# Tree stage of an eight-stage kernel: leaf nodes by gathered rows instead of dense products

## The reference, cut to what matters

```
logits = layernorm(x) @ W_in.T + b_in            # [tokens, 8 * 255]
acts   = silu(logits)
node 0 of each tree is visited; from a visited node the path goes left or right
by logits > 0, seven times; dmap is 1 at the eight visited nodes, else 0
x = x + (acts * dmap) @ W_out.T
```

## Time and profile before

| | us |
|---|---|
| median of 3 runs | 1630.63 (1630.32 to 1631.8) |
| profiled execution, its own time | 1630.92 |
| its span, first to last instruction | 1629.2 |
| PE busy | 1438.7 (88%) |
| DVE busy | 1072.1 (66%) |
| ACT busy | 755.6 (46%) |
| POOL busy | 116.5 (7%) |

### The profile page before, as it was taken

How to read it: one execution, slowest core, us unless ns; L and a number is a source line. 1 busy time by engine, 2 the same in 40 slices (tenths; PEclk the granted TensorE clock), 3 DMA queues, 4 the chain that set the end, 5 groups by cost and what they waited for, 6 DMA issues and landing times.

```text
span 1629.2 us, 26350 instructions
## 1 busy us (share of the span) xinstructions
PE 1438.7 (88%) x9842; PEld 1074.1 (66%) x9849; DVE 1072.1 (66%) x2358; ACT 755.6 (46%) x1264; POOL 116.5 (7%) x168
## 2 busy tenths in 40 slices
PE   7999999878897996799989999999988889999557
PEld 5666666557783443477786878787764677788446
DVE  4455575778877874687866465655458988886344
ACT  2211212257773666376672222222224877788323
POOL 1000000000000000111000000000010011001323
PEclk9999999989998997899998999999998999999779
DMA  9462202320000000000008910000100000010166
GB/s 323 167 207 78 78 1 78 127 85 14 14 3 0 1 1 1 25 14 1 14 2 265 303 43 1 1 1 0 33 7 7 1 7 2 7 31 24 41 186 180
DMA packets 60285, 96.62 MB, mean 59 GB/s; under 512 B 11091, under 2 KB 48972, under 8 KB 59982
## 3 DMA queue, kind: packets, MB, share of 16 engines
q1 hardware_dynamic: 57742, 78.50, 15.0%
q10 hardware_dynamic: 544, 12.16, 2.2%
q0 software_dynamic: 1872, 4.27, 0.7%
HBM read 73.21 MB, written 37.30 MB: 68 GB/s over the span
## 4 chain that ended last, share of the span: by engine, by line
PE 50%; issue 18%; DVE 15%; ACT 6%; DVEq 4%; DMA 2%; SPq 1%; POOL 1%; ACTq 1%; POOLq 1%
PE bank L1997 8%; PE bank L1998 8%; PE bank L1689 7%; PE bank L1667 7%; DVE MB L927 3%; PE bank L1794 3%; DVE plo L945 2%; PE bank L1845 2%; PE bank L1595 1%; PE bank L1765 1%; PE bank L1799 1%; PE bank L1798 1%; DMA jx<-copy_routed 1%; DVE raw L1211 1%; PE bank L1767 1%
## 5 line engine op out<-in xcount | busy, mean ns | idle before, releaser
L945 DVE TENSOR_TENSOR plo<-e,phi 120x512 f16<-120x512 f32 x256 | 179.1, 705 | 50.2 <-ACT phi L1419 46.5
L1413 ACT ACTIVATE e<-bank 120x512 f32<-120x512 f32 x256 | 150.6, 588 | 42.7 <-PE bank L1799 34.3
L927 DVE TENSOR_REDUCE MB<-bank 128x4 bf16<-128x480 f32 x256 | 155.9, 646 | 15.1 <-PE bank L1767 11.5
L1419 ACT ACTIVATE phi<-e 120x512 f16<-120x512 f32 x256 | 161.2, 630 | 8.8
L1344 ACT ACTIVATE act<-bank,bin 127x512 f32<-127x512 f32 x64 | 43.1, 687 | 167.2 <-DVE dec L757 163.2
L1667 PE MATMUL bank<-xT,winT 128*127 128x512 f32 (+1 forms) x256 | 114.6, 593 | 1.3 <-ACTq L1315 1.3
L1689 PE MATMUL bank<-woutT,msk 128*128 128x256 f32 (+1 forms) x512 | 115.1, 379 | 0.0
L676 DVE TENSOR_SCALAR high<-raw 128x512 int32<-128x512 int32 x96 | 41.0, 427 | 108.1 <-ACT raw L1548 60.9
L1689 PEld LDWEIGHTS bank<-woutT,msk 128*128 128x128 f32 (+1 forms) x512 | 96.8, 190 | 15.4
L556 POOL TENSOR_TENSOR veps<-mv,ceps 128x4 f32<-128x4 f32 x32 | 8.9, 278 | 1336.7 <-DVEq L647 1204.9
L1997 PE MATMUL bank<-hah,h1w 128*128 128x512 f32 x256 | 101.3, 396 | 3.6 <-DVE hal L679 3.6
(11 more groups left out here) (308 smaller groups left out, 3518.8 us busy)
## 6 DMA issues: line engine op xcount, KB each, us to landing
copy_routed<-zeros SPq DMA_DIRECT2D x1, 17028.0 KB
jw<-copy_experts SPq DMA_DIRECT2D x23, 385.0 KB, 3.3
seen<-in_h1T SPq DMA_DIRECT2D x8, 512.0 KB, 7.2
seen<-in_h2T SPq DMA_DIRECT2D x8, 512.0 KB, 4.9
h1w<-copy_h1T SPq DMA_DIRECT2D x1, 4096.0 KB, 16.7
h2w<-copy_h2T SPq DMA_DIRECT2D x1, 4096.0 KB, 14.3
ctxp<-in_ctxT SPq DMA_DIRECT2D x13, 240.0 KB, 3.0
jx<-copy_routed SPq DMA_DIRECT2D x23, 132.0 KB, 3.1
```

What stands on the lines that cost most here:

```text
L927: dve.tensor_reduce(MB[:, t, h0 // 8, SK + h0 % 8:SK + h0 % 8 + 4], b[:, 0:4 * SK].rearrange("p (h k) -> p h k", h=4), AX.X, ALU.max).then ...
L945: dve.tensor_tensor(plo[:, g % 3, :], e32[:, g % 3, :], phi[:, g % 3, :], ALU.subtract).then_inc(s.lo, 1)
L1413: act.activation(e32[:, g % 3, :], bank[2 + g % 3][0:SK, :], ACT.Exp).then_inc(s.exp, 1)
L1419: act.activation(phi[:, g % 3, :], e32[:, g % 3, :], ACT.Copy).then_inc(s.phi, 1)
```

## The change: what it does

The leaves leave PE. At the end of the first attention layer PE turns the leaf rows of `winT` and ACT writes them with the leaves' biases to a table in HBM (`leaves`, 1024 rows of 513 numbers: output weights, input weights, bias); SP copies the output weights into it. In the stage a running number g counts all 32 (pair, tree) steps. ACT turns the leaf counts into a one-hot map (`hot`); PE multiplies it with the leaf numbers (`leafn`), one column per tile; DVE adds the tree's offset and stores integers (`idx`); POOL gathers for each token its leaf's row into one of five buffers (`rowsG`). Three steps later DVE makes the dot of normalised row and gathered input weights (`leaf_logits`), ACT the silu (`leaf_values`), and DVE adds value times output weights to x (`add_leaves`) for all four tiles. The pair's inner sum is added to x five steps after its end, from banks 4 and 5 or 0 and 1 in turn. As the dots come late, the normalised rows have a second buffer (`xln_odd`). `low_bits` collects by an or of 1024 columns, with one reduction at the end. ACT issues the five weight copies in steps 3, 9, 14, 19 and 24. SP loads the first mask ahead of the stage. The last four steps (34 to 37) run inside the first four units of the attention, whose start no longer waits for the last residual. Six semaphores are shared with the last stage, whose waits count on from 32.

```
+STEPS, ROW, GB, LAG = PAIRS * TREES, 2 * D + 1, 5, 5
+SUMS = (4, 0)
...
+        for n0, n1 in ((0, 112), (112, INNER)):
+            sp.dma_start(woutT[n0:n1, :, :], nodes[n0:n1]).then_inc(ld_out_w, 16)
+        sp.dma_start(leaves[:, 0:D].rearrange("(t n) d -> n t d", n=LEAVES), nodes[INNER:NODES]).then_inc(leaf_rows, 16)
...
+        sp.dma_start(m32[:], a["mask"][0:TOK, :].rearrange("(t p) k -> p t k", p=128)).then_inc(mask_ready, 16)
...
+        def gather(g):
+            pool.wait_ge(Tf.row, g + 1)
+            if g >= GB:
+                pool.wait_ge(Tf.added, g - GB + 1)
+            for t in range(TT):
+                pool.indirect_dma_start(rowsG[g % GB][:, t, 0:ROW], None, leaves[:],
+                                        bass.IndirectOffsetOnAxis(idx[:, g % TREES, t:t + 1], 0),
+                                        bounds_check=TREES * LEAVES - 1, oob_is_err=False).then_inc(landed[g % GB], 16)
+        for i in range(PAIRS):
+            rstd_of(i + 2)
+        pool.wait_ge(leaf_rows, LEAF_ROWS)
+        for g in range(STEPS):
+            gather(g)
+            if g % TREES == 0:
+                rstd_of(g // TREES + (4 * 1 + 2))
...
-            dve.tensor_scalar(seen_low[:], seen[:, q, :].bitcast(I32), 0xFFF, None, ALU.bitwise_and)
-            dve.drain()
-            dve.tensor_reduce(lowmax[:, ds(i * SEEN + q, 1)], seen_low[:], AX.X, ALU.max)
+            if i == q == 0:
+                dve.memset(seen_low[:], 0)
+                dve.drain()
+            dve.tensor_tensor(seen_low[:], seen_low[:], seen[:, q, :].bitcast(I32), ALU.bitwise_or)
...
+        def decisions(g):
+            dve.wait_ge(Bf.logits, g + 1)
+            dve.tensor_scalar(dec0[0:INNER, g % 2, :], bank[2 + g % 2][0:INNER, :],
+                              negb[0:INNER, g % TREES:g % TREES + 1], None, ALU.is_gt).then_inc(Bf.dec, 1)
+        def masked(g):
+            dve.wait_ge(Bf.cnt, g + 1)
+            dve.wait_ge(Bf.act, g + 1)
+            dve.scalar_tensor_tensor(out=msk0[0:INNER, g % 2, :], in0=bank[6][0:INNER, :],
+                                     scalar=tgt[0:INNER, 0:1], in1=act0[0:INNER, g % 2, :],
+                                     op0=ALU.is_equal, op1=ALU.mult).then_inc(Bf.msk, 1)
+        def leaf_numbers(g):
+            dve.wait_ge(Tf.idx, g + 1)
+            dve.tensor_scalar(idx[:, g % TREES, :], bank[7][:, 0:TT], float(g % TREES * LEAVES), None,
+                              ALU.add).then_inc(Tf.row, 1)
+        def leaf_logits(g):
+            rows_in = (xln, xln_odd)[g // TREES % 2]
+            dve.wait_ge(landed[g % GB], got(g))
+            for t in range(TT):
+                if t == 2:
+                    dve.drain()
+                last = dve.scalar_tensor_tensor(out=dots[:, t % 2, :], in0=rows_in[:, t, :], scalar=1.0,
+                                                in1=rowsG[g % GB][:, t, D:2 * D], op0=ALU.mult, op1=ALU.mult,
+                                                accum_out=lv[:, g % GB, t:t + 1])
+            dve.drain().then_inc(Tf.dot, 1)
+        def add_leaves(g):
+            dve.wait_ge(Tf.val, g + 1)
+            if g == STEPS - 1:
+                dve.drain()
+            for t in range(TT):
+                xs = x[:, TT * (g // TREES) + t, :]
+                last = dve.scalar_tensor_tensor(out=xs, in0=rowsG[g % GB][:, t, 0:D], scalar=val[:, g % GB, t:t + 1],
+                                                in1=xs, op0=ALU.mult, op1=ALU.add)
+            last.then_inc(Tf.added, 1)
+        def tree_rows(i):
+            dve.wait_ge(xT_ps, 4 * 1 + i + 1)
+            dve.wait_ge(ln_rstd, i + (4 * 1 + 2))
+            for t in range(TT):
+                dve.tensor_scalar((xln_odd, xln)[i % 2][:, t, :], x[:, TT * next_pair(i) + t, :],
+                                  mv[:, t, 0:1], rstd[:, t:t + 1], ALU.subtract, ALU.mult)
+            dve.drain().then_inc(xln_ready, 1)
+        def tree_residual(i):
+            dve.wait_ge(Bf.out, i + 1)
+            dve.drain()
+            for h in range(2):
+                residual(i, h, bank[SUMS[i % 2] + h][:, :])
+            dve.drain().then_inc(res_done, 1)
         if phases > 1:
             dve.wait_ge(ld_in, LD_IN)
...
+                if g < STEPS and (p or not i):
+                    decisions(g)
+                if 1 <= g <= STEPS:
+                    masked(g - 1)
+                if 4 <= g < STEPS + 4:
+                    leaf_logits(g - 4)
+                if g == 2 * TREES:
                     weight_scales()
-                for p in range(TREES):
-                    dve.wait_ge(Bf.logits, i * (2 * TREES) + (2 * p + 1))
-                    dve.tensor_scalar(dec0[0:INNER, p % 2, :], bank[2 + 2 * (p % 2)][0:INNER, :],
-                                      negb[0:INNER, p:p + 1], None, ALU.is_gt).then_inc(Bf.dec, 1)
-                    if p >= 1:
-                        masked(p - 1)
-                    if p == 2:
+                if 1 <= g <= STEPS:
+                    leaf_numbers(g - 1)
+                if 5 <= g < STEPS + 5:
+                    add_leaves(g - 5)
+                if g < STEPS and not p and i:
+                    decisions(g)
+                if g >= TREES and g % TREES == LAG % TREES:
+                    tree_residual((g - LAG) // TREES - 1)
+                if g < STEPS:
+                    if p == 1:
                         norm_stats(1, i)
                     if p in (4, 6):
                         n, st, q = ((0, stage_w1, w1q), (1, stage_w2, w2q))[p // 2 - 2]
...
                         if i == 2 + n:
                             ternary(n, st, q)
                     if p == 3:
-                        norm_rows(1, i)
-                    for q in ((), (), (), (0, 1), (), (2, 3), (), (4, 5))[p]:
+                        tree_rows(i)
+                    for q in ((), (), (), (0,), (1,), (2,), (3,), (4, 5))[p]:
                         dve.drain()
                         if q == 0:
                             dve.wait_ge(ld_h1, i * LD_SEEN + LD_SEEN)
                         low_bits(i, q)
-                dve.drain().then_inc(Ff.low, 1)
-                masked(TREES - 1)
-                dve.wait_ge(Bf.out, i + 1)
-                for h in range(2):
-                    residual(i, h, bank[h][:, :])
-                dve.drain().then_inc(res_done, 1)
-            dve.tensor_reduce(lowall[:], lowmax[:], AX.X, ALU.max)
+                    if p == TREES - 1:
+                        dve.drain().then_inc(Ff.low, 1)
+            for g in range(STEPS + 2):
+                tree_step(g)
+            dve.tensor_scalar(seen_low[:], seen_low[:], 0xFFF, None, ALU.bitwise_and)
+            dve.drain()
+            dve.tensor_reduce(lowall[:], seen_low[:], AX.X, ALU.max)
             dve.drain().then_inc(Ff.low, 1)
...
+            if L is L1X:
+                dve.wait_ge(Tf.added, STEPS - GB + 1)
+            else:
+                dve.wait_ge(res_done, 4 * ph + 1)
...
+                    tree_step(STEPS + 2 + step + n)
...
+                if i >= 2:
+                    for j in range(2):
+                        act.wait_ge(leaf_ps, 2 * (i - 2) + j + 1)
+                        act.activation(table[:, 4 * (i - 2) + 2 * j:4 * (i - 2) + 2 * j + 2, 0:D],
+                                       bank[2 + j][:, :].rearrange("p (t d) -> p t d", t=2), ACT.Copy)
...
-        for w, copy in w_in.items():
-            act.dma_start(copy, a[w]).then_inc(w_copied, 16)
+        act.wait_ge(ld_in, LD_IN)
+        act.activation(table[:, :, D], bin2[:, :, 1], ACT.Copy)
+        act.drain().then_inc(leaf_ps, 1)
+        act.wait_ge(leaf_ps, 5)
+        act.dma_start(leaves[:, D:ROW].rearrange("(t n) c -> n t c", n=LEAVES), table[:]).then_inc(leaf_rows, 16)
...
+        def hot_leaves(g):
+            act.wait_ge(Bf.cnt, g + 1)
+            if g >= 2:
+                act.wait_ge(Tf.idx, g - 1)
+            act.activation(hot[:, g % 2, :], bank[7][:, :], ACT.Relu, bias=onec[:, 0:1]).then_inc(Tf.hot, 1)
+        def leaf_values(g):
+            act.wait_ge(Tf.dot, g + 1)
+            for t in range(TT):
+                last = act.activation(val[:, g % GB, t:t + 1], lv[:, g % GB, t:t + 1], ACT.Silu,
+                                      bias=rowsG[g % GB][:, t, 2 * D:ROW])
+            last.then_inc(Tf.val, 1)
...
+            def tree_step(g):
+                i, p = g // TREES, g % TREES
+                if g in (3, 9, 14, 19, 24):
+                    w, copy = copies[(3, 9, 14, 19, 24).index(g)]
+                    act.dma_start(copy, a[w]).then_inc(w_copied, 16)
+                if i and not p:
+                    evacuate_xT(i + (4 * 1 + 1), 2)
+                if g < STEPS and (p or not i):
+                    inner_values(g)
+                if 1 <= g <= STEPS:
+                    hot_leaves(g - 1)
+                if g < STEPS and not p and i:
+                    inner_values(g)
+                if 4 <= g < STEPS + 4:
+                    leaf_values(g - 4)
```

(53 more changed lines are left out.)

181 lines of the change are left out of this document (90 added, 91 removed).

## The result

The kernel after takes 1651.68 us (median of 4 runs, 1648.66 to 1657.75), the kernel before, beside it, 1631.22 (1630.32 to 1634.7). The ratio is 1.0117, with a 95% interval of 1.010 to 1.0134: slower by about 19 us, where 1641 was forecast (range 1611 to 1675). The profiled execution took 1652.8 us, its span is 1651.1, so 21.9 more than the profiled execution before.

The account below looks back on a forecast made before the run. PE was taken to bound the tree stage, DVE after the change. The profiled 1630.9 us plus 10.1 (attention's later start +1.2, leftovers +7.4 and +2.0, mask wait -0.5) gave 1641 us, range 1611 to 1675.

Parts of the forecast that it names:

- PE, from 7.33 to 4.2 us a tree, and DVE becomes the bound: Tree stage: leaf halves leave PE, some 100 us in all; DVE's tree costs more than PE's and sets the pace.
- Lean step 5.2 us: DVE's tree step without extra work: decision 0.66, mask product 0.66, dots 2.16, conversion 0.14, adds 1.56 us.
- rival A: DVE's new work is cheaper: port free (-8), sum's write hidden (-9), dots at 0.32 (-9); 1615 us; chance 0.32.
- Rival B: DVE's dot with its sum runs at half rate, 0.27 us more each, +34 us, 1675 us; chance 0.07.
- First four steps, 4.7 us each: Tree stage's start, without dots or adds, goes at a chain's pace; fifth decision 18.8 us after the first.
- Port, 8 us: Tree stage: contention of DVE and POOL over SBUF costs DVE one 0.23 us loss a tree, 8 us.
- POOL hides, DMA stalls 0: Tree stage: POOL's gather issues, 5.1 us a tree, hide under DVE's 7.0 us steps; gathers' landing costs nothing.
- Rival C: Two 4 MB copies in steps 14 and 19 hold gathers up, up to 10 us each; 1647 to 1661; chance 0.10.
- The sum of the stage: DVE's work from the fifth decision, 210.8 us, ends at 305.3, or 313.3 with the port's 8.
- Start, +1.8: Ahead of the tree stage, PE's sixteen transposes of leaf rows move the first logits from 71.90 to 73.7.
- The end, +7.4 ahead of the second low queries, +2 behind: Leftover dots and adds on DVE in the attention's first four units: 7.4 us before those queries, 2 after.
- Rival E: PE's clock falls to 1.2 GHz in the tree stage, 8.4 us a tree, +29 us, 1670 us; chance 0.03.

Follow-up runs that it names:

- e2: Kernel after with POOL's gathers replaced by plain loads of the same rows and bytes on ScalarE's queue; 1640.3 us, ratio 1.0033.
- e4: Kernel after with POOL's layer-norm step in the tree stage waiting for its sum by a semaphore, not a drain; 1642.5 us, ratio 1.0047.
- e5: Kernel after with the 11 MB of copies inside HBM sent as eleven 1 MB pieces, not five of 1 to 4 MB; 1660.1 us, ratio 1.0185.
- e11: e6 with the leaf adds shared, two tiles on PE by diagonals and two on DVE, and unused dot products stored as bf16; 1627.0 us, ratio 0.9960.
- e12: e11 with the stage's last four steps moved from the attention's first four units to its ninth to twelfth; 1627.1 us, ratio 0.9953.
- e1: Kernel after with SP issuing the second pair's mask and context loads ahead of the residual wait and 7 MB of weights; 1644.2 us, ratio 1.0062.
- e3: Kernel after without 23 of DVE's 24 low-bit passes; 1636.6 us, ratio 1.0007.
- e6: Kernel after with the edits of e1 and e4 together; 1638.0 us, ratio 1.0037.
- e10: e6 without 23 of DVE's 24 low-bit passes; 1627.0 us, ratio 0.9961.
- e8: Kernel before with SP issuing the 7 MB of gate and down weights only after the attention's fifth approximation; 1644.6 us, ratio 1.0080.
- e9: e6 with all leaf adds on PE by diagonals, at the end of its step, and unused dot products stored as bf16; 1631.4 us, ratio 0.9986.

## Why the prediction was right, point by point

Its verdict, its sign and its place for the approximations (331 forecast, 331.94 measured) were right, though several terms were off and cancelled. The agreement within 1 us is in part luck: 4.0 us of the start belong to the profiled execution (below), and without them the approximations would start at 328. The time is 11 us above the 1641 forecast, at the edge of the 1630 to 1652 that the forecast claimed for itself. One of its signs of being wrong came true: DVE waited for gathers before the dots, 4.3 us in two places. DVE is also busy for 85% of the stage and not over 90%. Its steps from the fifth decision on average 7.15 us, as against 7.0 forecast.

- *PE, from 7.33 to 4.2 us a tree, and DVE becomes the bound.* Right in kind: a step of PE without a wait takes 4.27 us (88.34 to 92.61), and DVE is busy for 85% of the stage. A group of four one-column products is 0.25 us long and takes 0.11 to the next start (88.23 to 88.34), instead of 0.3. PE's busy time in the stage fell by 72 us and not by 100: its records include tails, and the granted clock averages 0.89; this was not split. The stage was forecast at 239.6 us (73.7 to 313.3) and took 237.6.
- *Lean step 5.2 us.* It is 4.8. The term that was too dear is the dots: 1.74 us (102.00 to 103.74) instead of 2.16, about 13 us over 30 trees. The write of the sum shows as a row of 0.08 us, but the next dot starts in its shadow: start to start is 0.35. So of rival A's three cheap ends two nearly came true (the write hides; the port costs DVE nothing, below), and the third halfway: 0.35 lies between its 0.32 and the forecast's 0.39. Together they are worth 21 of A's 26 us; A's 1615 failed by what it shared with the forecast, the drain and the loads. Rival B is refuted: a dot with its sum takes 0.42 us. The Trainium skill (Vector Engine (DVE) Microarchitecture Reference, Points that are easy to get wrong) states that this form halves its throughput; the trace doesn't agree, and 0.35 from start to start is even less than the 0.39 of the form without the sum.
- *First four steps, 4.7 us each.* The first two decisions stand only 1.7 us apart (79.67, 81.38), the next 4.7 and 4.3 (86.07, 90.34); the fifth comes at 100.68, 21.0 behind the first and not 18.8, as the first wait for `rstd` (3.61 us) lies there.
- *Port, 8 us.* The step that failed in kind: e2 against after shows 0.5 us. The earlier trace rows showed one pair of subtractions 0.23 us longer, and that was carried to every tree. POOL's issues do take longer, 1.16 us in the mean and up to 2.30 instead of 1.00, and that is hidden. The Trainium skill (SBUF — State Buffer, Who interferes with whom) calls the port an exclusive lock; if it is at work in these runs, it is GpSimd that pays, as the dots keep their length; no run isolates what lengthens the issues.
- *POOL hides, DMA stalls 0.* Missing. The issues do hide, at 5.9 us a tree. But the prediction put down "some 2 us of layer-norm work per pair" for POOL and did not ask what the drain in it waits for behind four gathers: 11.2 us of the stage (e4). A gather lands after 4.2 us in the median, where 3 were left for it. Rival C had its one place (3.90 us at 184.41, behind a 4 MB copy, gone in e5) and not its size.
- *The sum of the stage.* 13 us too much for dots and 8 for the port, 11 too little for the drain; the remaining 8 us, so that the sum comes out 2 too long, are gaps of DVE that were not split further; two profiles of the same code (e11, e12) differ by 4.9.
- *Start, +1.8.* The sixteen transposes cost 0.87 and 0.88 us, as predicted. The other 4.0 us lie ahead of them: PE waits 0.86 us for its weights instead of 0.24, the product of these weights takes 3.78 us instead of 2.53, and the first keys and values take 5.79 us instead of 3.69, though the granted clock reads 1.00. The profiled executions of after, e1, e3, e6 and e10 have this last, largest part (5.4 to 6.2 us), those of before and the eight other kernels don't (3.69), among them e4 and e5, whose code up to there is that of after: it belongs to the execution, not to the change.
- *The end, +7.4 ahead of the second low queries, +2 behind.* Measured 6.7 (15.2 us from memset to these queries instead of 8.5) and, in e1, 3.4 behind: 10.0 instead of 9.4. Right. The 0.5 for the mask's wait was not won: 0.43 us of idling stand before the mask's use (317.23) in its place.
- *"Later stages keep their code apart from semaphore counts."* This sentence hid the other half of the loss, the path through SP's queue. SP's 7 MB wait for the same residual that moves 25 us back, and the mask and context behind them are wanted at a fixed distance from the approximations: 8 to 9 us (e1), 13 us where nothing else hides it (e8). The earlier trace rows showed SP's first mask load leaving behind the residual; what else left behind it was not followed.
- *Rival E.* The granted clock did fall, to 0.89 over the stage and 0.80 from 150 to 200 us. As DVE waited for PE's logits for only 2.6 us behind the fifth step, PE's gaps absorbed it.

Against 19 us by the ratio, the forecast's 10 are the leftovers; the loads are the other 9. What the stage gives (2.7 us) the transposes ahead of it take (1.8).

## What to carry to other kernels

When work moves past a completion count, list every queue that waits for this count, the one that issues loads first, and ask when each thing behind those loads is wanted; small loads that are wanted soon go ahead of big ones. While GpSimd has gathers under way, order a sum and its use by a semaphore and not by a drain. Taking 30 us of work from the busiest of four coupled engines gave 9 to 17 us here: before crediting such a cut in full, follow one step around the ring of engines, and see what is next in it.

## What the runs showed of the hardware that was not expected

- GpSimd's drain behind issued gathers ends 0.3 to 1.5 us after the last of them has landed: it holds for 3.66, 8.77, 4.78 and 6.53 us in the four places; with a semaphore in its place (e4) the two operations are 0.08 us apart.
- An issue on SP's queue behind 7 MB took 9.6 to 9.7 us, in the kernels before, after and e8 alike.
- A 128x256 dot with its sum takes 0.42 us, 0.35 from start to start, and is not slowed by gathers beside it (425 against 421 ns).
- PE stood still for 5 to 6 us at single places (from 114.8 in e10, near 1517 in e9) with no wait that explains it in the profile. No run tried the cause.
